# Linear attention and routed experts on one core: the state's sums in 32-row tiles right behind a tile's scores, with the masks, norm tails and opening moved

## The chip, the cores and the metric

The kernel runs on one core of a Trainium2 chip. The metric is the device time of one execution in microseconds; lower is better. The times given are medians of several executions.

## The reference

A block of a transformer on 4 sequences of 2048 rows of 256 numbers, in fp32. Two norms are modulated by vectors worked out from a condition (`mod = silu(c) @ wmod`, six vectors for each sequence). The first half is causal linear attention with 16 heads of 16 numbers, the second a mixture of 8 experts of which each row takes two, with at most 1280 rows for an expert.

```
h = layernorm(x) * (1 + ca) + sa
q, k, v = split(h @ w_qkv.T);  q, k = elu(q) + 1, elu(k) + 1
for each position t:  S += k_t v_t^T;  z += k_t;  o_t = (S^T q_t) / max(z . q_t, 1e-6)
x = x + ga * (o @ w_out.T)
h = layernorm(x) * (1 + cb) + sb
gates = top 2 of softmax(h @ w_router.T), rows past an expert's capacity dropped, weights normalised
x = x + gb * sum_e gate_e * (silu(h @ w_gate.T) @ w_down[e].T)
```

## The kernel before

The rows are cut into 64 tiles of 128 rows, and 4 tiles make a group. The attention part is one loop over slots n (`run_slots`), written out once for each engine: in slot n an engine does its share of tile n, and beside it a quarter of the projections of the next group (stage 1) and of the routing of a group two behind (`routing`: "columns", "first", "second", "place" in the slots 0 to 3 of a group). An order in each engine's `slot_` is written by hand, and semaphores join them. The first 8 slots are negative ones, with an `early` hook for setup work. Behind the attention part comes an expert part of 40 steps, which the change leaves alone.

In a slot TensorE's order is: scores of the tile (`scores`, L1368, 16 calls of 32 rows by 64 columns of weights and 128 moving columns, in the four banks of SCW), transposes of the heads of the tile before and of the keys of the next one (`columns_and_keys`, L1380 and L1386), in slot 0 the transposes of h2 (L1533), a quarter of the projections (L1501 or L1511), the sums from the state (`from_state`, L1398, 8 calls of 64 by 128), the state update (`add_to_state`, L1445, 8 calls of 64 by 64 with 68 moving columns), the sums from the tile (`from_tile`, L1412, 32 calls of 64 by 17), in slot 0 logits (L1552) and stage 1's transposes (L1485), then the output product (L1472), the transposes of the head sums (`head_rows`, L1460) and the other part of the projections. An fp32 product of one call is two records in the trace.

A tile has two halves of 64 rows; the state Sbd is kept for each half. The sums from the state and those from the tile are one accumulation, in OB, which lies in the columns of the same four banks in which the scores stood. So the sums may start only when VectorE has read the scores (`masked_scores`, L994, semaphore sm_done), and the scores of the next tile only when ScalarE has read OB (ot_done). State update: TensorE writes keys times values of both halves to PM, VectorE masks the blocks that belong to one head (L1025, Snew, 272 numbers in a row, semaphore state_read) and adds the halves to the state (L1030, L1036, 136 numbers; sbd_done). PM's banks also hold other results: logits (L1552) and `head_rows` wait for state_read, and in slot 0 the state update waits for ScalarE's two copies of h2's columns (L830, h2t_done).

VectorE's order in a slot is: masks, in slot 0 the row statistics of a group to come (L1059), in slot 2 that norm's tail (`ln_tail`, L1049 to L1052), the state, phi of the projections (L1043), the residual addition (L1159), the normalised heads (`normalise_heads`, L1003 to L1010, An), row statistics (L1163), and in slot 0 the tail of the second norm. The function `between` puts single steps of the routing (`choose`, `place`) among them; place has 9 steps, all in slot 3. GpSimd takes a norm's tail further (L572), modulates the rows (L500, L506), and sends them to their experts (L514); a send waits for a named step of TensorE.

In the opening the modulation vectors come from two products (`modulation`, L1345), the second of them just ahead of slot -1. They are written to the banks of the scores, and VectorE takes them out from slot -1 on (L968 to L979), so that the first scores wait for that; SP sends them to memory and back in all rows (MB), behind the loads of the groups 2 to 7.

## Time and profile before

| | |
|---|---|
| median of 3 executions | 843.34 us (842.8 to 853.23) |
| profiled execution | 848.72 us, its span 847.0 us |
| mean granted TensorE clock | 0.966 |
| TensorE busy | 788.7 us, 93% |
| VectorE / ScalarE / GpSimd busy | 577.3 / 478.8 / 484.0 us |
| first scores of the attention part | 30.12 us into the span |

The profiled execution is one of the longer ones; differences are worked out in its own rows and then set against the median. Busy shares are means over stages, so the rows below are of single stretches and slots.

### The profile page before, as it was taken

What the parts mean: (1) busy time and instruction counts of PE and PEld (TensorE: products, weight loads), DVE (VectorE), ACT (ScalarE), POOL (GpSimd) and SP (SyncE); (2) the same over time, 40 slices, a digit from 0 to 9 for tenths busy, and PEclk for the clock granted to TensorE, in tenths of its full rate; (3) what the DMA queues carried; (4) which work ended last, traced back from release to release, by engine and by line L of the source; (5) the groups of instructions that cost most, each with busy time, mean ns of one, the idle gap of its engine ahead of it and who ended that gap; (6) DMA issues with size and microseconds to landing.
All of it is one profiled execution on the core that took longest, in us unless ns stands there. A gap on an engine that the chain in (4) does not pass through costs nothing.

```text
span 847.0 us, 30958 instructions
## 1 busy us (share of the span) xinstructions
PE 788.7 (93%) x12583; PEld 688.8 (81%) x12583; DVE 577.3 (68%) x1869; ACT 478.8 (57%) x941; POOL 484.0 (57%) x621
## 2 busy tenths in 40 slices
PE   6899899999999999999999998878999997999994
PEld 4687778877877877877877876678999997999993
DVE  4577487878777877877877777522766646767762
ACT  4566467666667667667667664233554553554541
POOL 2203154656666776675766655462765746666764
PEclk9999799999999999999999999759999998999997
DMA  7409823142344132231021121014676655677653
GB/s 282 167 4 337 244 78 115 53 140 77 115 144 136 55 138 90 76 119 68 36 81 54 49 75 39 18 51 150 127 162 147 137 129 112 145 158 158 121 96 38
DMA packets 66844, 95.76 MB, mean 113 GB/s; under 512 B 7682, under 2 KB 48642, under 8 KB 66584
## 3 DMA queue, kind: packets, MB, share of 16 engines
q1 hardware_dynamic: 34136, 50.26, 18.9%
q0 software_dynamic: 21760, 31.66, 16.7%
q10 hardware_dynamic: 10816, 11.96, 4.5%
q8 instruction: 97, 1.59, 0.8%
q14 instruction: 35, 0.29, 0.1%
HBM read 38.97 MB, written 63.36 MB: 121 GB/s over the span
## 4 chain that ended last, share of the span: by engine, by line
PE 77%; DVE 9%; issue 5%; POOL 4%; DMA 3%; ACT 1%; POOLq 0%; SPq 0%; DVEq 0%; ACTq 0%
PE SCW L1727 12%; PE SCW L1398 8%; PE SB L1472 7%; PE SCW L1742 6%; PE SCW L1412 5%; PE PM L1501 5%; PE PJ L1501 3%; PE PM L1445 3%; PE SCW L1368 3%; PE SB L1742 3%; PE PM L1742 3%; PE PJ L1511 3%; PE PM L1460 3%; PE PM L1380 2%; PE PM L1511 2%
## 5 line engine op out<-in xcount | busy, mean ns | idle before, releaser
L514 POOL DMA_INDIRECT slot_rows<-Hrow,sloti x128 | 131.6, 1028 | 102.9 <-PE SCW L1412 60.2
L632 POOL DMA_INDIRECT out<-EX,desti x80 | 125.3, 1566 | 24.2 <-POOL idle L460 11.3
L460 POOL TENSOR_TENSOR idle<-mhalf 128x1 f32<-128x1 f32 x136 | 60.2, 443 | 76.3 <-DVE EX L1298 46.7
L994 DVE TENSOR_TENSOR Sm<-SCW,tri 128x512 f32<-128x512 f32 x128 | 82.1, 682 | 25.7 <-PE SCW L1368 23.9
L851 ACT ACTIVATE OTs<-SCW 128x512 f32<-128x512 f32 x64 | 38.3, 598 | 84.4 <-PE SCW L1412 84.4
L1398 PEld LDWEIGHTS SCW<-QT,Sbd 64*128 64x128 f32 x1024 | 65.3, 192 | 18.7 <-issue 18.0
L564 POOL TENSOR_TENSOR hT<-Sm,hT 128x512 fp32r<-128x512 f32 x30 | 38.3, 1278 | 67.4 <-ACT hT L686 66.6
L1398 PE MATMUL SCW<-QT,Sbd 64*128 64x64 f32 x1024 | 73.8, 284 | 3.0 <-DVE Sm L994 2.8
L701 ACT ACTIVATE N<-X,nb,rs 128x256 f32<-128x256 f32 x128 | 66.3, 592 | 7.5 <-POOL nb L574 4.8
L892 ACT ACTIVATE VA<-SCW 128x512 f32<-128x512 f32 x80 | 47.9, 598 | 38.5 <-PE SCW L1727 35.3
L1742 PE MATMUL SCW<-w_qkv,QS 128*128 128x256 f32 x416 | 62.9, 287 | 4.4 <-DVE QS L1270 4.4
L1025 DVE TENSOR_TENSOR Snew<-PM,headmask 128x272 f32<-128x272 f32 x64 | 28.2, 441 | 52.9 <-PE PM L1445 52.6
L1727 PE MATMUL SCW<-VS,w_g 128*128 128x256 f32 x480 | 61.5, 284 | 0.0
L1727 PE MATMUL SCW<-KS,w_g 128*128 128x256 f32 x480 | 61.4, 283 | 0.0
L1742 PEld LDWEIGHTS SCW<-w_qkv,QS 128*128 128x128 f32 x416 | 57.3, 193 | 4.6 <-issue 4.6
L1727 PEld LDWEIGHTS SCW<-VS,w_g 128*128 128x128 f32 x480 | 58.0, 189 | 0.0
L1727 PEld LDWEIGHTS SCW<-KS,w_g 128*128 128x128 f32 x480 | 57.8, 188 | 0.2 <-DVE KS L1262 0.2
L788 ACT ACTIVATE QM<-QT,parity 128x256 f32<-128x256 f32 x128 | 57.7, 502 | 0.0
L572 POOL TENSOR_TENSOR rs<-vp,mhalf 128x4 f32<-128x4 f32 x31 | 32.5, 1048 | 41.3 <-DVE vp L1052 40.9
L1159 DVE TENSOR_TENSOR X<-X,SB 128x256 f32<-128x256 f32 x64 | 26.7, 418 | 41.2 <-PE SB L1472 40.6
L1412 PE MATMUL SCW<-Sm,VA 64*17 64x64 f32 x4096 | 54.0, 222 | 0.0
L1501 PE MATMUL PJ<-hT,w_qkv 128*128 128x512 f32 x192 | 52.8, 410 | 0.3 <-ACT hT L686 0.3
(253 smaller groups left out, 2025.8 us busy)
## 6 DMA issues: line engine op xcount, KB each, us to landing
Hrow<-slot_rows SPq DMA_DIRECT2D x32, 516.0 KB, 4.4
slot_rows<-erow ACTq DMA_DIRECT2D x1, 10400.0 KB, 41.5
X<-x SPq DMA_DIRECT2D x16, 512.0 KB, 4.8
out<-X SPq DMA_DIRECT2D x16, 512.0 KB, 3.2
QT<-slot_rows SPq DMA_DIRECT2D x8, 516.0 KB, 3.8
Hrow<-MB SPq DMA_DIRECT2D x8, 512.0 KB, 3.5
MB<-mod_rows SPq DMA_DIRECT2D x1, 2048.0 KB
slot_rows<-Hrow,sloti POOLq DMA_INDIRECT x128
```

The source lines that it names most:

```text
L460: pool.tensor_tensor(idle[:, k:k + 1], mhalf[:, 0:1], mhalf[:, 0:1], ALU.add).then_inc(breath, 1)
L514: pool.indirect_dma_start(xe, bass.IndirectOffsetOnAxis(sloti[:, par, k, t:t + 1], 0), Hrow[:, par, t, :], None, bounds_check=last_slot, o ...
L632: pool.indirect_dma_start(out, bass.IndirectOffsetOnAxis(desti[s % 2][:, a:a + 1], 0), Ys[s % 2][:, a, :], None, bounds_check=TOK - 1, oob ...
L701: act.activation(dst, X[:, xt, :], ACT.Identity, scale=rs[:, t:t + 1], bias=nb[:, t:t + 1]).then_inc(s_ready, 1)
L788: act.activation(QM[:, (n + 1) % 2, odd], QT[:, g1 % 2, :, q1 * P:(q1 + 1) * P], ACT.Copy, scale=parity[:, odd:odd + 1]).then_inc(q_masked, 1)
L994: dve.tensor_tensor(Smh(T % 2)[:, 2 * b:2 * b + 2], SCW[:, 2 * b:2 * b + 2, 0:2 * P].rearrange("p r (m i) -> p r m i", i=CH), tri64[:].uns ...
L1398: mm(OB[:, k, b, cc, :], Sbd[part(b), (2 * T + k) % 4, cc, :], QT[part(b), gp, cc, q * P + CH * k:q * P + CH * k + CH], start=(cc == 0), s ...
L1412: last = mm(OB[32 * a:32 * a + SW, k, b, cc, :], VA[part(k), gp, q, head(cc, r, s), :], Smh(T % 2)[part(k), r, 2 * cc + s, :], start=False ...
L1472: last = mm(SB[:, 0:D], ATs[:, cc, :], w_ogs[T // TPB % 2][:, cc, :], start=(cc == 0), stop=(cc == DC - 1))
L1501: last = mm(PJ[m % 2][:], w_qkv[:, wp, cc, (m + 2) % 4 * P:((m + 2) % 4 + 1) * P], hT[:, hp, cc, :], start=(cc + i == 0), stop=(cc == DC - ...
L1727: last = mm(SC[hh][:, (f % 2) * BW:(f % 2 + 1) * BW], w_g[:, wp, cc, f * P:(f + 1) * P], XT[par][:, xp, cc, :], start=(cc + i == 0), stop= ...
L1742: last = mm(((MA, KR), (MD, SB))[par][a][:, 0:D], hid[par][hp][:, f, a * P:(a + 1) * P], WD[k][wp][:, f, :], start=(f + i == 0), stop=(f = ...
```

## The change

The state's sums get columns of their own in the four banks (256 to 383, OB), and are made in tiles of 32 rows and 64 columns with two heads each: 16 calls, right behind the scores of their tile. As two row tiles of the array then write to one bank, the second half of them waits until the scores have run (scores_run). sc_full, for which the masks and some of GpSimd's sends wait, is now given by the last of the sums, and the wait for the masks stands ahead of the sums from the tile. The state has two heads in a block instead of four: Sbd, Snew, headmask and the update's moving operand have half the width, the update has 16 calls of 64 by 32 with 34 moving columns. On VectorE the tail of the second norm goes from the end of slot 0 to behind the masks of slot 1; the last three steps of place go to behind the masks of the next slot 0; and in slot 3 no routing step stands inside `normalise_heads`. In the opening both modulation products run at j = 4, ahead of the first projections, VectorE takes them out there, the masks' setup goes from j = 0 to j = 2, the first statistics wait for a semaphore of one memset instead of all constants, and SP sends MB ahead of the loads of the groups 4 to 7.

```diff
-        OB = SCW[:, :, 0:DC * CH].rearrange("p (k b) (c i) -> p k b c i", k=2, c=DC)
+        OB = SCW[:, :, 2 * P:2 * P + DC * CH].rearrange("p (b k) (c i) -> p k b c i", k=2, c=DC)
...
-            for g in range(2, EARLY):
+            for g in range(2, 4):
                 load_rows_of(g)
...
+            for g in range(4, EARLY):
+                load_rows_of(g)
...
             dve.memset(VA[:], 1.0).then_inc(dve_setup, 1)
+            dve.wait_ge(ones_set, 1)
+
             def early(j):
-                if j == 0:
+                if j == 2:
                     dve.wait_ge(consts, N_CONST)
...
-
-                if j == 7:
 
                     dve.wait_ge(mod_mm, 3)
                     dve.tensor_copy(mod12[:, 0:2, :], OBm).then_inc(gate_fix, 1)
...
-                        if step == "place" and k < 9:
+                        if step == "place" and k < (9 if n >= TILES - 3 else PLACED):
                             place(g, k)
...
                 if tile_ok(n):
                     masked_scores(T)
+                if q == 1 and group_ok(gn - 1):
+                    dve.wait_ge(bn2, 4 * gn)
+                    ln_tail(st2, mv2, vp2, nm2, ag2, vpe2, gn)
+                if step == "columns" and group_ok(g - 1):
+                    for k in range(PLACED, 9):
+                        place(g - 1, k)
...
                 if tile_ok(n):
-                    normalise_heads(T, between, between)
+                    if step == "place":
+                        normalise_heads(T, lambda: None, lambda: None)
+                    else:
+                        normalise_heads(T, between, between)
...
-                if q == 0 and group_ok(gn - 1):
-                    dve.wait_ge(bn2, 4 * gn)
-                    ln_tail(st2, mv2, vp2, nm2, ag2, vpe2, gn)
...
                 if j == 4:
                     modulation(0)
-                if j == 6:
                     modulation(1)
...
-                last.then_inc(sc_full, 1)
+                last.then_inc(scores_run, 1)
...
                 pe.wait_ge(sbd_done, T + 1)
-                for k in range(2):
-                    pe.wait_ge(sm_done, 2 * T + k + 1)
+                for other in range(2):
+                    if other:
+                        pe.wait_ge(scores_run, T + 1)
                     for cc in range(DC):
-                        for b in range(2):
-                            mm(OB[:, k, b, cc, :], Sbd[part(b), (2 * T + k) % 4, cc, :],
-                               QT[part(b), gp, cc, q * P + CH * k:q * P + CH * k + CH], start=(cc == 0), stop=False,
-                               skip_group_check=True)
+                        for r in range(4):
+                            rows, half = slice(32 * r, 32 * r + 32), slice(64 * (r % 2), 64 * (r % 2) + 64)
+                            k = (r + other) % 2
+                            last = mm(OB[half, k, r // 2, cc, :],
+                                      Sbd[rows, (2 * T + k) % 4, cc, :, :].rearrange("p s w -> p (s w)"),
+                                      QT[rows, gp, cc, q * P + CH * k:q * P + CH * k + CH], start=(cc == 0), stop=False,
+                                      skip_group_check=True)
+                last.then_inc(sc_full, 1)
...
+                pe.wait_ge(sm_done, 2 * T + 2)
...
-                        for b in range(2):
-                            h = head(cc, 2 * b, 0)
-                            last = mm(PM[part(b), k, cc * QH * SW:(cc + 1) * QH * SW],
-                                      Kn[part(k), cc * P + CH * b:cc * P + CH * b + CH],
-                                      VA[part(k), gp, q, h:h + QH, :].rearrange("p s w -> p (s w)"),
+                        for r in range(4):
+                            h = head(cc, r, 0)
+                            last = mm(PM[32 * r:32 * r + 32, k, cc * 2 * SW:(cc + 1) * 2 * SW],
+                                      Kn[part(k), cc * P + 32 * r:cc * P + 32 * r + 32],
+                                      VA[part(k), gp, q, h:h + 2, :].rearrange("p s w -> p (s w)"),
                                       start=True, stop=True, skip_group_check=True)
...
-                if tile_ok(n) and n > 0:
-                    scores(n)
+                if tile_ok(n):
+                    if n > 0:
+                        scores(n)
+                    from_state(n)
...
-                if tile_ok(n):
-                    from_state(n)
```

## Rows read from the trace of the kernel before

**Rows 1.** Busy time by stretch: span, PE, PEld, DVE, ACT, POOL, clock, DMA.

```profile
200.00:300.00 100.00, 97.95 (x2036) 80.20 (x2018) 77.78 (x278) 67.31 (x143) 66.36 (x88) 1.00 0.34 117
```

**Rows 2.** The waits from 60 to 450 us: total, times, longest.

```profile
PE PM L1380 <- DVE An L1010: 8.2, 18, 1.2
```

**Rows 3.** Timeline of a slot 3: start, length, engine, line, operation.

```profile
250.57 0.69 PE L1368 MATMUL SCW<-QM,KT 32*64 32x128 f32 x32
...
251.19 0.44 PE L1380 MATMUL PM<-ident,An 128*128 128x128 f32 x2
...
251.37 1.29 DVE L994 TENSOR_TENSOR Sm<-SCW,tri 128x512 f32<-128x512 f32 x2 [0.83 <-PE SCW L1368]
...
253.28 1.11 PE L1398 MATMUL SCW<-QT,Sbd 64*128 64x64 f32 x16
...
254.32 0.47 PE L1445 MATMUL PM<-VA,AK 64*64 64x68 f32 x16
...
254.72 0.83 PE L1412 MATMUL SCW<-Sm,VA 64*17 64x64 f32 x64
```

**Rows 4.** Groups by line from 40 to 450 us: busy us, mean ns, idle before.

```profile
L1398 PE MATMUL SCW<-QT,Sbd 64*128 64x64 f32 x816 | 58.1, 282 | 1.9 <-DVE Sm L994 1.6
...
L1412 PE MATMUL SCW<-Sm,VA 64*17 64x64 f32 x3264 | 42.8, 221 | 0.0
...
L1368 PE MATMUL SCW<-QM,KT 32*64 32x128 f32 x1632 | 35.6, 280 | 2.2 <-issue 2.2
...
L1445 PE MATMUL PM<-VA,AK 64*64 64x68 f32 x816 | 24.1, 234 | 0.0
...
L1030 DVE TENSOR_TENSOR Sbd<-Sbd,Snew 128x136 f32<-128x136 f32 x51 | 19.6, 385 | 0.6
...
L1152 DVE TENSOR_TENSOR Hrow<-gk,esum 128x8 f32<-128x8 f32 x11 | 1.9, 173 | 0.4
```

**Rows 5.** Timeline of the slot 0 behind it.

```profile
258.36 0.69 PE L1368 MATMUL SCW<-QM,KT 32*64 32x128 f32 x32
...
260.69 1.39 DVE L1059 BATCH_NORM_STATS2 st<-X 128x6 f32<-128x256 f32 x4
260.74 0.60 ACT L830 ACTIVATE h2T<-PM 128x512 f32<-128x512 f32 x1
...
261.62 0.47 PE L1445 MATMUL PM<-VA,AK 64*64 64x68 f32 x16
...
262.15 0.44 DVE L1025 TENSOR_TENSOR Snew<-PM,headmask 128x272 f32<-128x272 f32 x1
...
262.77 0.64 PE L1552 MATMUL PM<-h2T,w_r 128*32 128x128 f32 x16
```

**Rows 6.** Timeline of the slot 1 behind it.

```profile
265.69 0.69 PE L1368 MATMUL SCW<-QM,KT 32*64 32x128 f32 x32
...
268.22 1.28 DVE L994 TENSOR_TENSOR Sm<-SCW,tri 128x512 f32<-128x512 f32 x2
...
269.05 1.17 PE L1398 MATMUL SCW<-QT,Sbd 64*128 64x64 f32 x16 [0.16 <-DVE Sm L994]
```

**Rows 7.** Timeline of a slot 0 in which An is late.

```profile
164.21 0.41 PE L1380 MATMUL PM<-ident,An 128*128 128x128 f32 x2 [1.15 <-DVE An L1010]
```

**Rows 8.** Timeline of the opening.

```profile
13.17 3.57 PE L1345 MATMUL SCW<-Sm,cS 128*4 128x512 f32 x4
...
22.77 1.88 PE L1345 MATMUL SCW<-Sm,cS 128*4 128x512 f32 x4
...
28.73 0.67 DVE L968 COPY Hrow<-SCW 4x512 f32<-4x512 f32 x1
...
30.12 0.70 PE L1368 MATMUL SCW<-QM,KT 32*64 32x128 f32 x32 [2.48 <-DVE Hrow L970]
```

**Rows 9.** Timeline of slot 0 of group 2.

```profile
94.82 0.47 PE L1368 MATMUL SCW<-QM,KT 32*64 32x128 f32 x15 [2.20 <-issue]
```

**Rows 10.** Busy time of the stretch around it, columns as in rows 1.

```profile
92.00:107.00 15.00, 12.21 (x181) 9.62 (x179) 4.09 (x11) 6.87 (x14) 1.03 (x1) 0.66 0.63 187
```

More of the change, by code:

```diff
@@ L50 @@
 EARLY = 8
+PLACED = 6
 BIG = 1.0e5
@@ L79, in adaln_block @@
         EX = sb("EX", [P, 2, GW])
-        Snew = sb("Snew", [P, 2, DC * QH, SW])
+        Sbd = sb("Sbd", [P, 4, DC, 2, VW])
+        Snew = sb("Snew", [P, 2, DC * 2, SW])
         OTs = sb("OTs", [P, 2, DC, 2, CH])
@@ L148, in adaln_block @@
             Sm = attention.enter_context(nc.sbuf_tensor("Sm", [P, 2, H, P], F32))
-            Sbd = attention.enter_context(nc.sbuf_tensor("Sbd", [P, 4, DC, QH * VW], F32))
         QS = sb("QS", [P, 2, FC, BW], F32R)
@@ L218, in adaln_block @@
         wipe = sem("wipe")
+        ones_set = sem("ones_set")
         c_silu = sem("c_silu")
@@ L241, in adaln_block @@
         q_masked = sem("q_masked")
+        scores_run = sem("scores_run")
         sc_full = sem("sc_full")
@@ L450, in _ @@
                                base=0, channel_multiplier=-1).then_inc(consts, 1)
[L452 removed]
+            pool.affine_select(out=pairmask[:], in_=pairmask[:], pattern=[[-2 * DH, GT]], compare_op=ALU.is_ge,
                                fill=0.0, base=0, channel_multiplier=1).then_inc(wipe, 1)
             pool.wait_ge(wipe, 1)
[L455 removed]
+            pool.affine_select(out=pairmask[:], in_=pairmask[:], pattern=[[2 * DH, GT]], compare_op=ALU.is_ge,
                                fill=0.0, base=DH - 1, channel_multiplier=-1).then_inc(consts, 1)
@@ L1024, in state @@
                 at_least(dve, sbd_done, t)
-                dve.tensor_tensor(Snew[:], PM[:, :, 0:DC * QH * SW].rearrange("p k (h w) -> p k h w", h=DC * QH),
-                                  headmask[:].unsqueeze(1).to_broadcast([P, 2, DC * QH, SW]), ALU.mult
+                dve.tensor_tensor(Snew[:], PM[:, :, 0:DC * 2 * SW].rearrange("p k (h w) -> p k h w", h=DC * 2),
+                                  headmask[:].unsqueeze(1).to_broadcast([P, 2, DC * 2, SW]), ALU.mult
                                   ).then_inc(state_read, 1)
```

32 lines of the change are left out of this document (13 added, 19 removed).

## Prediction

> **What bounds the kernel now.** I read the windows first. In a steady stretch of the attention part TensorE is busy 97.95 us of 100 at a full clock, VectorE 77.78 [rows 1]. So what counts is how long TensorE's own list of a tile takes, and its few waits. The waits name one of size: the transposes of the normalised heads (L1380) stand 8.2 us in 390 behind VectorE's An, 18 times [rows 2]. The timeline of a slot gives the steps of a tile from start to start [rows 3]: scores 0.62 us (250.57 to 251.19), sums from the state 1.04 (253.28 to 254.32), state update 0.40 (254.32 to 254.72). The groups by line give the mean of one record [rows 4], so the spacing inside a step is (busy - mean) / (count - 1): sums from the state (1.11 - 0.282) / 15 = 0.055 us, state update (0.47 - 0.234) / 15 = 0.016, scores (0.69 - 0.280) / 31 = 0.013, sums from the tile (0.83 - 0.221) / 63 = 0.010. What a step takes beyond count times spacing (1.04 - 16 x 0.055 = 0.16; 0.40 - 16 x 0.016 = 0.15; 0.62 - 32 x 0.013 = 0.20) is the drain where the next step has another tile shape. The sums from the state are dear: 16 records at 0.055, with 64 rows by 128 columns of weights.
>
> **Sums from the state in 32-row tiles.** Calls go from 8 to 16 a tile, records from 16 to 32; each is 32 rows by 64 columns, and four array tiles are in turn. The old state update has the same 64 columns of weights, four array tiles and almost the same moving length (68 for 64): 0.016 us a record. So the step is 32 x 0.016 = 0.50 us. The scores ahead have the same 32*64 shape, so no drain stands between. Scores and sums together: 0.42 + 0.50 + one drain 0.20 = 1.12 us. The new wait on scores_run stands between the two halves. Behind it on TensorE is everything; what it waits for is the end of the last score, at 0.69 us from the slot's start, and the masks now show 0.11 us from such an end to a start on another engine (251.26 to 251.37) [rows 3]: released at 0.80. The first half of the sums covers it until 0.42 + 0.25 = 0.67. Exposed: 0.13 us; bounds 0 (all covered) and 0.3 (the second half starts with an empty array, the first spacing of a step again). I take 0.15, so 1.27 us where 0.62 + 1.04 = 1.66 stood: **0.39 less** a tile.
>
> **State update.** 32 records of 64*32 with 34 moving columns, where 16 of 64*64 with 68 stood. The nearest row is the sums from the tile (same shape, 0.010 a record): 32 x 0.010 = 0.31, and no drain behind it, since that step follows. 0.40 becomes 0.27 to 0.31, and with the initial spacing of the next step saved I take **0.16 less**; bounds 0.1 and 0.2. VectorE's read of it, Snew (0.44 us for 272 elements [rows 5]), has 136, and the two additions half as many: off TensorE's path except in slot 0, below; there I count 0.1.
>
> **The waits that go or come.** L1380 now starts 1.27 us after the scores instead of 0.62, so An has that much longer: the 8.2 us go where An is the last: 0.22 us in each slot 1 (12 times, 2.6), the other 5.6 in the slots 0, 1.15 in the one shown [rows 7]. The masks start when the sums end: 1.27 - 0.20 + 0.28 + 0.11 = 1.4 us into the slot, take 1.29 and end at 2.7. Only the sums from the tile wait for them now, and these come at 3.6 in slots 1 to 3 (1.27, columns 0.4, a projection 1.6, update 0.3). Slack 0.9; no cost. The new early wait of the sums for the state of the tile before (sbd_done) is met: Snew and two additions of 0.385 [rows 4] end 1.8 us behind the update's start (261.62 to 263.4), and the next scores start at 265.69 [rows 5, 6]; 2.3 us of slack, in slot 3, where place steps stand between, some 1.5.
>
> **Slots 2 and 3:** 0.39 + 0.16 = 0.55 less each. **Slot 1** has now the norm tail ahead of the masks: sc_full is there 0.80 us behind the slot's start, at 266.5, the masks start at 268.22 and the sums wait for them (0.16, and the step is 1.17 for 1.11) [rows 6]. The tail behind the masks takes that and the An wait away: 0.16 + 0.06 + 0.22 = 0.45, so 0.55 + 0.45 = 1.0 less. The tail moves from 1.4 to 2.7 us into the slot and ends at 3.5; queued behind it on VectorE are a choose step and Snew, which has until the update at 3.6. GpSimd's power step stands behind a send that waits for sc_full anyway, so it moves by little.
>
> **Slot 0 gives back.** Today the 8 transposes of h2 (1.0 us) and then the sums (1.04) cover ScalarE's two copies of it (the second ends at 261.34), and the update starts at 261.62 [rows 5]. With the sums gone ahead, everything up to the second copy is 0.65 later (end 3.6 us into the slot), TensorE has nothing from 2.8 on, and the update starts at 3.75 instead of 3.26. Then the second thing: logits wait for state_read, that is for VectorE's Snew. VectorE has in line masks (1.4 to 2.7), the three moved tail steps of place (three chained small steps of 173 ns [rows 4] with their waits, 0.6, to 3.3), row statistics 1.39 (to 4.75), Snew 0.33 (to 5.1). Logits start at 5.25 instead of 262.77 - 258.36 = 4.41: **0.85 more**. Against it stands An's wait in the slots 0, 5.6 us / 12 = 0.45 in the mean: normalise_heads no longer has place steps between its own, and L1380 is later. But where An is late, so are the masks and Snew, so I count half: 0.85 - 0.25 = **+0.6**.
>
> **The sum.** A group: -0.55 - 0.55 - 1.0 + 0.6 = -1.5 us. Thirteen groups (3 to 15, the last without projections): -19.5. The first three, without logits in two: -1.8 each, -5.5. The **opening**: the second modulation product (1.88 us) moves ahead of the first projections, where the first product took 3.57 us, so it costs there between 1.88 and 3.57 (I take 2.0, near its price at 22.77, since it is the later part of a longer run of work); it leaves 22.77, and parity and masks leave the path to the first norm (0.7). VectorE's seven steps (from 28.73 on, 3.5 us) go under the projections, and the 2.48 us that the first scores wait for them go [rows 8]. -0.7 + 2.0 - 1.9 - 2.5 = -3, with part of VectorE's phi work then late: bounds -4.5 and -1. SP's rows of groups 4 to 7 now queue behind the modulation rows; they are first read some 30 us later, cover enough. Together -28 us: 848.7 of the profiled execution becomes 820.7. That run lies 5.4 over the median of three, 843.3, so the median becomes **815**.
>
> **Rivals.**
> 1. *The wait moves to VectorE.* If the handshake costs 0.3 and VectorE's line in slot 0 is longer than counted (GpSimd's tensor steps stretch VectorE's additions of 0.30 to 0.7 and more; their mean is 0.385 for it [rows 4]), slot 0 gets +1.4 and each slot 0.15 less: group -0.55 - 0.55 - 1.0 + 1.4 + 0.6 = -0.1. With the opening: about 838. For it: slot 0's times are all on one line. Against: GpSimd sends, and does not compute, in that half of slot 0. Chance 0.16, within 2%.
> 2. *Records have a floor.* If a record with little work costs no less than the 0.025 us that the state update takes now per record (0.40 / 16), sums and update are 0.80 each for 1.04 + 0.40, less 0.2 of drain: nothing gained in slots 2 and 3, 0.45 in slot 1, +1.1 in slot 0: some +10 us less the opening, 850. The 4096 records at a spacing of 0.010 speak against it [rows 4]. Chance 0.03. The Trainium skill (TensorEngine Tiling, Instruction Overhead) says that a matmul with a free dimension of 1 takes as long as one of 60 and that no tiling factor should come from a dimension that is already small; 34 moving columns offend against that.
> 3. *Slower: instruction supply.* In one slot TensorE stood 2.20 us in the middle of a tile's scores with nothing to wait for, and the 15 us around it have a mean granted clock of 0.66 [rows 9, 10]: 2.2 + 15 x 0.34 = 7 us lost. The change adds 16 calls a tile, some 16% more TensorE records in less time. If that starves it, each stop costs 7 us; from four more stops the -28 are gone, at seven it is +21: 865. It happened once in 64 tiles. Chance 0.05. One stop more alone gives 822, one less 808.
> 4. *More than forecast.* If the statistics in slot 0 finish before I count, slot 0 loses only 0.2 and the handshake is free: group -2.4, 800. Chance 0.10.
> 5. *The reordering does nothing*, the 32-row tiles running one after another at 0.055: 32 x 0.055 = 1.76, +0.72 a tile, 860 and more. The scores run 32*64 tiles at 0.013 [rows 4]. Chance 0.02.
>
> **How the numbers follow.** The forecast, 815, has 0.64, with 806 to 826 for its own bounds. The range 802 to 838 leaves out rivals 2, 3, 5 and half of 4. Two per cent is 17 us, about what a measurement of this kernel can tell from no change: faster means under 826.5, which holds the forecast and rival 4, 0.74; within 2% rivals 1, 2 and part of 3, 0.20; slower 0.06.
>
> **What would show it.** Sums from the state: 32 records, the first 0.45 us into the slot. Scores to L1380: 1.27 us. Slots 2 and 3 near 7.15 us, slot 1 near 7.5, slot 0 near 8.2, with L1552 behind Snew and L1445 behind the copies to h2T. L1380 no longer behind An in the waits. First scores near 28 us. I would be wrong if L1412 waits for the masks, if slot 0 grows by over 1.5 us, or if the second half of the sums starts over 0.3 us behind the first.

## The result and the profile after

The changed kernel takes **840.1 us** at the median of 20 runs, the kernel before 845.0 beside it: a ratio of **0.9935**, 95% interval 0.9909 to 0.9962. That is a gain of some 5 us (5.5 by the ratio, 4.9 by the medians): real, but under one per cent. The forecast was 815, 28 us less, with a range of 802 to 838; the result lies outside it. Ratios here and below leave out executions over 1.5% longer than the fastest of their kernel, medians keep them. The profiled execution went from 848.7 to 842.6 us, its span from 847.0 to 840.8.

The page of the changed kernel, its busy line and its chain of work:

```profile
PE 762.5 (91%) x14631; PEld 673.3 (80%) x14631; DVE 551.9 (66%) x1869; ACT 482.2 (57%) x941; POOL 488.2 (58%) x621
...
PE 77%; issue 8%; POOL 5%; DMA 4%; DVE 3%; ACT 2%; POOLq 0%; SPq 0%; ACTq 0%; DVEq 0%
```

TensorE is busy 26 us less (788.7 before), and the time is only 6 us less: 20 us came back as idle time. The chain says where to look: 8% of it is "issue", time in which the engine waited for nothing that the profile shows (5% before). The windows and the waits from 60 to 450 us, as in [rows 1, 2]:

```profile
200.00:300.00 100.00, 95.25 (x2531) 79.00 (x2529) 74.83 (x286) 69.82 (x146) 70.00 (x91) 1.00 0.37 127
```

```profile
PE PM L1457 <- ACT h2T L833: 10.6, 12, 0.9
PE PM L1457 <- issue: 7.4, 12, 0.7
PE SCW L1424 <- issue: 2.9, 2, 2.7
PE PM L1386 <- issue: 2.0, 1, 2.0
PE PM L1497 <- issue: 1.8, 1, 1.8
PE SCW L1374 <- issue: 1.8, 1, 1.8
```

The wait for An, 8.2 us in [rows 2], is gone but for 0.6 us. In its place stand two waits of the state update (L1457), each 12 times, and single stops of 1.8 to 2.7 us. The first wait was forecast (h2T). The second, 0.6 us each, is called "issue", but its length and its count, once in each slot 3, ask for a name. The timeline of slot 3 (scores L1374, sums from the state L1407, An's transposes L1386, projection of V L1523, update L1457, sums from the tile L1424, output L1484) has it, when ScalarE's row is laid beside TensorE's:

```profile
247.97 0.69 PE L1374 MATMUL SCW<-QM,KT 32*64 32x128 f32 x32
248.46 0.79 PE L1407 MATMUL SCW<-QT,Sbd 32*64 32x64 f32 x32
249.19 0.44 PE L1386 MATMUL PM<-ident,An 128*128 128x128 f32 x2
...
251.31 0.60 ACT L807 ACTIVATE VA<-PJ 128x512 f32<-128x512 f32 x1 [0.83 <-PE PJ L1523]
...
252.00 0.36 PE L1457 MATMUL PM<-VA,AK 64*32 64x34 f32 x32 [0.60 <-issue]
252.22 0.87 PE L1424 MATMUL SCW<-Sm,VA 64*17 64x64 f32 x64
253.02 1.13 PE L1484 MATMUL SB<-Sm,AK 128*128 128x256 f32 x4
```

The update starts 0.09 us behind the end of ScalarE's copy of V (251.91), and `add_to_state` waits for that copy when the next tile is the first of a group. So this "issue" is a wait for ScalarE. Slot 0 behind it:

```profile
258.92 0.60 ACT L833 ACTIVATE h2T<-PM 128x512 f32<-128x512 f32 x1
...
259.67 0.36 PE L1457 MATMUL PM<-VA,AK 64*32 64x34 f32 x32 [0.88 <-ACT h2T L833]
259.91 1.35 PE L1424 MATMUL SCW<-Sm,VA 64*17 64x64 f32 x64
...
260.11 1.06 POOL L517 DMA_INDIRECT slot_rows<-Hrow,sloti  x1 [0.51 <-issue]
...
260.42 0.30 DVE L1026 TENSOR_TENSOR Snew<-PM,headmask 128x136 f32<-128x136 f32 x1
...
261.19 0.64 PE L1564 MATMUL PM<-h2T,w_r 128*32 128x128 f32 x16
```

The sums from the tile take 1.28 us here until the next step starts, 0.76 in the kernel before and 0.80 in the slot above. The slot 1 behind it has no wait left:

```profile
264.11 0.69 PE L1374 MATMUL SCW<-QM,KT 32*64 32x128 f32 x32
...
267.42 0.36 PE L1457 MATMUL PM<-VA,AK 64*32 64x34 f32 x32
267.66 0.86 PE L1424 MATMUL SCW<-Sm,VA 64*17 64x64 f32 x64
```

The stops stand each in the middle of a step; of the five of 1.8 us or more, at 34.8, 71.6, 85.4, 101.9 and 356.0 us, three:

```profile
71.63 0.37 PE L1386 MATMUL PM<-ident,An 128*128 128x128 f32 x1 [1.96 <-issue]
...
85.41 0.83 PE L1424 MATMUL SCW<-Sm,VA 64*17 64x64 f32 x38 [2.68 <-issue]
...
101.89 0.92 PE L1374 MATMUL SCW<-QM,KT 32*64 32x128 f32 x23 [1.83 <-issue]
```

A balance of both traces, in us, from the starts of the scores of tiles 0, 4, 12, 60 and 63 (slots in the middle: mean from one start of scores to the next, over the 12 slots of a kind among n = 12 to 59):

| | before | after | difference | forecast |
|---|---|---|---|---|
| first scores at | 30.12 | 27.77 | -2.3 | -3 |
| n0 to n3 | 31.9 | 33.8 | +1.9 | -1.8 |
| n4 to n11 | 69.0 | 71.7 | +2.7 | -3.6 |
| n12 to n59 | 380.5 | 370.1 | -10.4 | -18 |
| of it a slot 0 | 7.76 | 8.27 | +0.51 | +0.6 |
| a slot 1 | 8.47 | 7.34 | -1.13 | -1.0 |
| a slot 2 | 7.69 | 7.27 | -0.42 | -0.55 |
| a slot 3 | 7.79 | 7.96 | **+0.17** | **-0.55** |
| n60 to n62 | 26.0 | 24.6 | -1.4 | -1.5 |
| behind them | 309.4 | 312.9 | +3.4 | 0 |

Some 22 us are missing: 9 of them in the slots 3 from n12 on, 10 in the first 12 slots, 3 at the end. The experiments go after each. All ratios below are to the kernel before. Slot means ("in the mean") are over the 12 slots of a kind among n = 12 to 59; single slots are named.

### The profile page after: what moved, and what is told of

Same layout as the page of the kernel before. It is cut to its first block, busy times and chain, and to the rows that moved or that the text cites. A ratio compares the mean times of both kernels' runs of the same rounds, so it can differ in the third digit from the quotient of the medians.

```text
span 840.8 us, 35024 instructions
## 1 busy us (share of the span) xinstructions
PE 762.5 (91%) x14631; PEld 673.3 (80%) x14631; DVE 551.9 (66%) x1869; ACT 482.2 (57%) x941; POOL 488.2 (58%) x621
## 4 chain that ended last, share of the span: by engine, by line
PE 77%; issue 8%; POOL 5%; DMA 4%; DVE 3%; ACT 2%; POOLq 0%; SPq 0%; ACTq 0%; DVEq 0%
PE SCW L1739 11%; PE SB L1484 7%; PE SCW L1424 6%; PE SCW L1754 6%; PE PJ L1513 5%; PE PM L1513 5%; PE SCW L1374 5%; PE SCW L1407 4%; PE PM L1472 3%; PE PJ L1523 3%; PE PM L1754 3%; PE SB L1754 3%; PE PM L1457 2%; PE PM L1386 2%; PE PM L1523 2%
## 5 line engine op out<-in xcount | busy, mean ns | idle before, releaser
L517 POOL DMA_INDIRECT slot_rows<-Hrow,sloti x128 | 135.5, 1058 | 60.4 <-issue 28.4
L1424 PE MATMUL SCW<-Sm,VA 64*17 64x64 f32 x4096 | 64.2, 223 | 6.6 <-issue 5.4
L1739 PE MATMUL SCW<-KS,w_g 128*128 128x256 f32 x480 | 63.1, 289 | 0.0
L1424 PEld LDWEIGHTS SCW<-Sm,VA 64*17 64x17 f32 x4096 | 51.8, 93 | 12.0 <-issue 9.0
L800 ACT ACTIVATE AK<-PM 128x512 f32<-128x512 f32 (+1 forms) x66 | 38.7, 586 | 39.3 <-PE PM L1392 38.4
L1513 PE MATMUL PM<-hT,w_qkv 128*128 128x512 f32 x192 | 53.9, 417 | 0.0
```

Of the source, the lines that this page charges most:

```text
L517: pool.indirect_dma_start(xe, bass.IndirectOffsetOnAxis(sloti[:, par, k, t:t + 1], 0), Hrow[:, par, t, :], None, bounds_check=last_slot, o ...
L1424: last = mm(OB[32 * a:32 * a + SW, k, b, cc, :], VA[part(k), gp, q, head(cc, r, s), :], Smh(T % 2)[part(k), r, 2 * cc + s, :], start=False ...
L1513: last = mm(PJ[m % 2][:], w_qkv[:, wp, cc, (m + 2) % 4 * P:((m + 2) % 4 + 1) * P], hT[:, hp, cc, :], start=(cc + i == 0), stop=(cc == DC - ...
L1739: last = mm(SC[hh][:, (f % 2) * BW:(f % 2 + 1) * BW], w_g[:, wp, cc, f * P:(f + 1) * P], XT[par][:, xp, cc, :], start=(cc + i == 0), stop= ...
```

## The experiments

**Slot 3.** The sums from the tile need only the masks, and these end at 2.7 us; so they can cover the copy of V.

```diff
+                if q == 3 and tile_ok(n):
+                    from_tile(n)
                 if n >= -1 and tile_ok(n + 1):
                     add_to_state(n, g, routed, step)
-                if tile_ok(n):
+                if q != 3 and tile_ok(n):
                     from_tile(n)
```

> Changed kernel with one step moved: in slot 3 alone the sums from the tile run ahead of the state update, so that their 0.8 us cover ScalarE's copy of the V projection. Theory A (the cover that the sums from the state gave to that copy is what slot 3 lost): slot 3 goes from 7.95 us to 7.25, 15 slots, 10 us less than the changed kernel, about 0.982 of the kernel before. Rival B (the gain is lost to stops in TensorE's instruction supply and a fuller VectorE, not to this wait): the next waits take it over, slot 3 stays over 7.7, under 3 us less, about 0.990. Rival C: the masks end too late for the earlier place (they end 2.7 us into the slot, the sums from the tile would start at 3.3), so it costs nothing.

Measured: 830.9 us, **0.9834** (0.9789 to 0.988). Slot 3 has a mean of 7.29 us. Its rows:

```profile
247.62 0.60 ACT L807 ACTIVATE VA<-PJ 128x512 f32<-128x512 f32 x1 [0.83 <-PE PJ L1523]
...
247.65 0.83 PE L1424 MATMUL SCW<-Sm,VA 64*17 64x64 f32 x64
248.33 0.41 PE L1457 MATMUL PM<-VA,AK 64*32 64x34 f32 x32
248.67 1.13 PE L1484 MATMUL SB<-Sm,AK 128*128 128x256 f32 x4
```

The copy runs from 247.62 to 248.22 beside the sums, and the update does not wait. Theory A has it: exchanging two calls gives more than the whole change gave.

**The sums from the state back at the old place in slots 0 and 3** (`LATE` true for q = 0 and 3). Here VectorE's masks wait for `scores_run`, and the sums for the masks, since both use the same banks.

```diff
                     if n > 0:
                         scores(n)
-                    from_state(n)
+                    if not LATE(q):
+                        from_state(n)
...
+                if LATE(q) and tile_ok(n):
+                    pe.wait_ge(sm_done, 2 * n + 2)
+                    from_state(n)
                 if n >= -1 and tile_ok(n + 1):
```

> Changed kernel with the sums from the state (still in 32-row tiles) back at their old place in slots 0 and 3, behind the masks and ahead of the state update; slots 1 and 2 as changed. Theory A (the placement loses in slots 0 and 3 what the small tiles gain, since ScalarE's copies of h2 and of V lose their cover): slot 3 goes from 7.95 to 7.25 and slot 0 from 8.06 to 7.4, 15 x 0.7 + 13 x 0.65 = 19 us less than the changed kernel, about 0.971 of the kernel before. Rival B (slot 0 is set by VectorE's row statistics and Snew, whatever TensorE does): slot 0 stays at 8.0, 10 us less, about 0.982. Rival C (stops in the instruction supply grow with any faster stretch): under 5 us less.

Measured: 831.9 us, 0.9833 (0.9797 to 0.9868), less than half of what theory A gives. Slot 3 came down to 7.47. Slot 0 is 7.50 at its best (n12, n32), but 8.29 in the mean: the waits from 120 to 500 us hold L1391 behind An again, 6.1 us in 7 waits, up to 1.3 each. So the early sums hide a late An; putting them back uncovers it.

**The old place in all slots** (`LATE` true for every q).

> Changed kernel with the sums from the state, in 32-row tiles, at the old place in all slots; only the tile form, the norm tail, the place steps and the opening are changed then. If the placement gives nothing by itself, slots 1 and 2 stay at 7.25 to 7.4 (the handshake of 0.15 goes, one more drain of 0.15 to 0.2 comes) and the time is that of the version with two slots moved back, 0.97 to 0.975 of the kernel before. If the placement is what gains in slot 1 and 2 (no wait for An), these are 0.2 to 0.4 longer each, 30 slots, 6 to 12 us more than that version.

Measured: 855.2 us, **1.0124** (1.0087 to 1.0162), outside all that was expected: slots 1 and 2 are 8.41 and 7.73 us. In the rows of a slot 1 (n33) the 32 sums from the state take 0.63 us, as they should, but the sums from the tile 1.23, beside a send of GpSimd's:

```profile
307.09 1.30 PE L1429 MATMUL SCW<-Sm,VA 64*17 64x64 f32 x64
...
307.23 0.99 POOL L522 DMA_INDIRECT slot_rows<-Hrow,sloti  x1 [1.63 <-PE SCW L1412]
...
308.32 1.13 PE L1489 MATMUL SB<-w_og,AK 128*128 128x256 f32 x4
```

GpSimd's sends wait for `sc_full`, which the change moved from the end of the scores to the end of the sums; with the sums late, a send is released right ahead of the small records. In slot n10 of the same run, where no group is sent yet, the same step takes 0.78. That asks for the send to be moved alone. The changed kernel shows the same by degrees: a slot 2 has 0.64 us of a send beside its sums from the tile, and they take 0.93 us in nearly all of them, a slot 3 has none and takes 0.80. The send is moved first in slot 0 of the changed kernel:

```diff
                 if paced and q == 0:
+                    pool.wait_ge(state_read, T + 2)
                     send_row(0, 0)
```

> Changed kernel with GpSimd's first send of a slot 0 held until VectorE has read the state (Snew). Theory (the send, which the moved place steps have pushed from the slot's first 2 us onto the state update and the sums from the tile, slows TensorE's small records there: 64 of them take 1.22 us from groups 3 on, 0.79 without a send): the logits come 4.7 instead of 5.14 us into slot 0, 12 slots, 5 us less, 0.987. Rival (the 64 records are slow because they follow a wait and 32 others, whatever GpSimd does): logits at 5.14, 0.9935.

Measured: 829.9 us, **0.9817** (0.9762 to 0.9872). The logits come at 4.68 us in place of 5.14 (4.7 was expected) and a slot 0 without a late An or a stop is 7.60 long instead of 8.06. Twelve of these are 5.5 us; the means of slot 0, 7.95 for 8.27, give 3.8, with a stop of 1.8 us in n20 of this trace. By the medians it is 10 us, more than the trace explains. The rows of n32:

```profile
289.45 0.82 PE L1425 MATMUL SCW<-Sm,VA 64*17 64x64 f32 x64
290.24 0.65 PE L1565 MATMUL PM<-h2T,w_r 128*32 128x128 f32 x16
...
290.48 1.07 POOL L517 DMA_INDIRECT slot_rows<-Hrow,sloti  x1 [1.37 <-DVE Snew L1027]
```

Then in the version with the sums late everywhere, with the sends of slots 1 and 2 back where the kernel before had them:

```diff
-                    pool.wait_ge(sc_full, T + 1)
+                    pool.wait_ge(scores_run, T + 1)
                     send_row(1, 0)
```

(and the same ahead of `send_row(2, 1)`)

> The version with the sums from the state in 32-row tiles at their old place in every slot, and GpSimd's sends of slots 1 and 2 released by the end of the scores, as in the kernel before, where they were released by the end of the sums, 0.2 us ahead of the state update. Theory (a send that runs beside the 32 and 64 small records of the update and the sums from the tile slows them by 0.43 us): the sums from the tile take 0.79 us again in slots 1 and 2, which go from 8.41 and 7.73 us to 8.0 and 7.3, 24 slots, 10 us less: 1.000 of the kernel before instead of 1.012. Rival (the 64 records are slow because 64 small ones stand right ahead of them): no change, 1.012.

Measured: 840.7 us, **0.9943** (0.9909 to 0.9977). That is better than the 1.000 expected: one semaphore's name is worth 1.8% of that version. Slots 1 and 2 go from 8.41 and 7.73 to 8.14 and 7.24 in the mean; the mean of slot 1 holds a stop in n29 (11.71); n13, n33 and n37 are 7.68.

```profile
306.31 0.99 POOL L522 DMA_INDIRECT slot_rows<-Hrow,sloti  x1
...
307.64 0.85 PE L1429 MATMUL SCW<-Sm,VA 64*17 64x64 f32 x64
308.42 1.13 PE L1489 MATMUL SB<-w_og,AK 128*128 128x256 f32 x4
```

0.78 us with the send over ahead of it, 1.23 beside it. The rival, that 64 small records behind 64 others are slow, falls: they stand in the same row here. The two traces also tell the send's row on GpSimd from its transfer. The packets of the sends (the profile's queue "software_dynamic") run beside the 0.78 us here, 22 of them between 307.64 and 308.42, and none runs beside the 1.23 us of the run before, from 307.09 to 308.32. So the stretching goes with the send's row, and not with the data on its way. Other work of GpSimd's does not do it either: a TENSOR_TENSOR of 1.06 us, from 307.32, stands beside the 0.78 us here.

The two runs also price the early place itself. A slot 2 has 7.16 us with the sums late and no send beside the small records, 7.12 with them early (n10) and 7.27 with them early and a send: nothing to gain. A slot 1 has 7.68 for 7.25, 0.43, which is mostly its wait for An.

**Slot 0's other waits.** Sums from the tile ahead of the update in slot 0 too:

> Changed kernel with the sums from the tile ahead of the state update in slots 0 and 3 (the run before had it in slot 3 alone). If slot 0 is set by the logits' wait for VectorE's Snew, which stands behind 1.4 us of row statistics, filling TensorE's wait for the copies of h2 gives nothing: the update still starts near 3.7 us into the slot, the logits near 5.15, slot 0 stays at 8.05. If instead TensorE's wait for the copies (0.88 us) is what slot 0 lost, slot 0 goes to 7.3.

Measured, one execution: 823.2 us. Neither of the two came: slot 0 is 7.67 without a late An (8.18 in the mean), the logits start at 4.75. Then VectorE's statistics behind Snew as well:

```diff
-                if q == 0 and group_ok(gn + 2) and gn >= 1:
-                    ln1_stats(G, gp)
...
                     state(n, between, lambda: None)
+                if q == 0 and group_ok(gn + 2) and gn >= 1:
+                    ln1_stats(G, gp)
```

> As the run before, and VectorE's row statistics of slot 0 (1.4 us) moved behind Snew and its two additions. Theory (slot 0 is two waits, one behind the other: the update for ScalarE's copies, the logits for Snew behind the statistics): the logits start near 4.45 us into the slot instead of 5.15, slot 0 goes from 8.05 to 7.35, 13 x 0.7 = 9 us less than with slot 3 alone put right: about 822 us, 0.972 of the kernel before. Rival: the later statistics make VectorE late in slot 1 or the next An late, and half of it comes back: 0.977.

Measured: 823.8 us, 0.9709 (0.9607 to 0.9811), but not for the reason given: Snew starts 4.40 us into n32, 4.41 in the run ahead.

```profile
280.75 0.30 DVE L1026 TENSOR_TENSOR Snew<-PM,headmask 128x136 f32<-128x136 f32 x1 [1.20 <-PE PM L1457]
...
281.10 0.64 PE L1564 MATMUL PM<-h2T,w_r 128*32 128x128 f32 x16 [0.74 <-DVE Snew L1026]
```

VectorE is idle for 1.20 us ahead of Snew, waiting for the update, which by its row began at 280.00. In the run ahead the statistics ended just when the update was done; moving them gave nothing. My theory for this edit fell. With the send held as well (and the fill in pieces, last experiment) Snew comes at 4.15 to 4.18 and the logits at 4.50 in the slots without a late An: 0.52 us behind the update's start where it was 0.75 with the send beside it, so the send seems to stretch the update too.

**The stops.** What a stop waits for stands among the DMA transfers, in the queue that the profile calls "instruction": 97 transfers of 16 KB in the kernel before, 113 in the changed one. The stop that ends at 85.41 has one in it, from 83.03 to 84.08. The view of the DMA queues from 82.73 to 85.41 has:

```profile
q8 instruction: 1, 0.02, 2.4%
```

It ends 1.33 us ahead of the stop's end; for the stops at 34.8, 71.6, 101.9 and 356.0 it is 1.46, 1.48, 1.52 and 1.63. In the traces of all runs there are 75 stops of over 1.0 us named "issue" between 30 and 515 us, and 73 of them end 1.2 to 1.7 us behind the end of such a transfer (the other two, 2.0 and 2.5, stand in the narrow fill below). So in the stops TensorE waits for instructions. In the five of the changed kernel the transfer itself takes 0.9 to 1.1 us, no longer than elsewhere: it comes late and not slowly, and what made it late the traces don't show.

A stop can cost more than its length. Right behind the stop of 2.68 us, in which TensorE was idle, the granted clock is 0.50, the lower of the two levels (1.2 GHz); so it is behind those at 34.8, 71.6 and 101.9, and not behind the one at 356.0:

```profile
85.00:91.50 6.50, 6.09 (x52) 4.48 (x51) 1.61 (x5) 1.39 (x3) 5.26 (x10) 0.50 1.09 333
```

The stops between 58 and 104 us lie in the 10.65 MB fill of the expert rows, one transfer. It was cut into ten, one in each of the slots 1 to 10, in both kernels.

```diff
+                if 1 <= n <= 10:
...
+                    act.dma_start(fill[:, 8 * n - 8:8 * n, :], erow[:].to_broadcast([P, 8, D + 4])).then_inc(init_out, 16)
```

> Changed kernel with the 10.5 MB fill of the expert rows sent in ten pieces, one in each of the slots n = 1 to 10, where one transfer stood at n = 3. Theory A (TensorE's instructions are fetched late while the fill takes all queues, and that makes the stops of 2 to 2.7 us between 69 and 102 us): the stops of over 1.5 us there go, slots n5, n6 and n8 come from 10.64, 12.81 and 11.23 to 8 or less, 8 to 11 us less: 0.982 to 0.985 of the kernel before. Rival B (the stops come from the instructions themselves, wherever they are fetched): the same number of stops, same time. Rival C: the pieces spread the stops over ten slots, no gain.

> Kernel before with the same ten pieces. Theory A: it had two stops in that stretch and slot n8 of 14.88 us; with the pieces n8 comes to about 8, 6 to 7 us less: 0.992. If the changed kernel gains 3 us or more on top of that by the same edit, the change pays more for the fill than the kernel before did. Rival: equal gains in both, so the fill is no part of what the change missed.

Measured: the changed kernel 834.7 us, 0.987 (0.9807 to 0.9933); the kernel before 839.9, 0.9919 (0.9881 to 0.9957). So some 5.5 and 7 us: equal within the intervals, so that by the times alone the rival of the second text stands. The traces say why. In the kernel before no stop is left, n4 to n11 take 61.8 us instead of 69.0. In the changed one they take 66.8 instead of 71.7, and three stops remain, 1.68 us in n6 (at 75.7) and these two, in n6 and n10:

```profile
81.76 0.61 PE L1424 MATMUL SCW<-Sm,VA 64*17 64x64 f32 x38 [2.15 <-issue]
...
113.55 0.77 PE L1424 MATMUL SCW<-Sm,VA 64*17 64x64 f32 x57 [1.78 <-issue]
```

Next the fill as one transfer, but of the last four columns of each row alone: as many pieces, 0.16 MB.

```diff
-                    act.dma_start(xe[:, 0:D + 4].rearrange("(p n) r -> p n r", p=P),
-                                  erow[:].to_broadcast([P, SLOTS // P, D + 4])).then_inc(init_out, 16)
+                    act.dma_start(xe[:, D:D + 4].rearrange("(p n) r -> p n r", p=P),
+                                  erow[:, :, D:D + 4].to_broadcast([P, SLOTS // P, 4])).then_inc(init_out, 16)
```

> Changed kernel with a fill that writes only the last four columns of each expert row (weights, index, mark) instead of all 260: 0.16 MB for 10.65, as one transfer at the same place; the rest of a row that nobody sends is never stored. Theory A (the stops between 58 and 102 us are instruction fetches that wait behind the fill's bytes): no stop of over 1.5 us between 60 and 130 us, the slots n4 to n11 take 61 us together instead of 71.7, 9 us less in all: 0.983 of the kernel before. Rival B (the stops belong to the instructions and come at other places too): n4 to n11 over 66 us, stops near n6 and n10 as with the ten pieces, 0.988.

> Kernel before with the same narrow fill. Theory A: n4 to n11 take 61.8 us as with the ten pieces (69.0 with the whole fill), no stops: 0.991. The difference between the two kernels in these eight slots is then what the change gains there when nothing disturbs it, and the difference with the whole fill what the fill took of it; if the changed kernel gains 2 us or more beyond what this one gains, part of the missed gain is the fill's.

Measured: the changed kernel 836.2 us, 0.988 (0.9832 to 0.9928), the kernel before 848.0, 1.0016 (0.998 to 1.0052). The bytes are gone and the stop is not. It is one now, in n5 of both, and longer in the changed kernel (first fence) than in the one before (second):

```profile
75.90 0.37 PE L1386 MATMUL PM<-ident,An 128*128 128x128 f32 x1 [5.89 <-issue]
```

```profile
76.74 0.62 PE L1412 MATMUL SCW<-Sm,VA 64*17 64x64 f32 x28 [3.10 <-issue]
```

The length is not the changed kernel's own, for in the best version below, with the same fill, the one stop there is 2.5 us. So the fill does not need its bytes to hold TensorE; many small pieces do it too, and theory A, as written, was wrong. That it is the number of pieces in one transfer fits the ten parts, but no run varied that number alone. The other seven slots of the changed kernel are undisturbed in that run (67.2 - 15.4 = 51.8 us); with n5 at the 7.12 that it takes with the ten pieces, n4 to n11 would be 58.9. Against 61.8 in the kernel before that is 2.9 less, near the forecast's 3.6. The whole fill thus took 71.7 - 58.9 = 12.8 us of the changed kernel and 69.0 - 61.8 = 7.2 of the kernel before in the two profiled executions, and the difference, 5.6, is most of the miss of 6.3 in these slots. The two prices come out of the rows: three stops are 6.5 us, and a mean granted clock of 0.87 over the 46 us from 58 to 104 costs some 46 x 0.13 = 6.0 us (my estimate, as if all of it went by the clock), 12.5 in all; in the kernel before 2.2 us of a stop and 46 x 0.09 = 4.1. The same windows of the changed kernel, the kernel before, and the kernel before with ten pieces; the clock is the third number from the end:

```profile
58.00:104.00 46.00, 37.46 (x893) 30.64 (x885) 21.63 (x69) 23.67 (x46) 11.22 (x19) 0.87 0.88 269
```

```profile
58.00:104.00 46.00, 42.23 (x878) 34.58 (x877) 28.30 (x77) 26.78 (x52) 12.06 (x19) 0.91 0.88 268
```

```profile
58.00:104.00 46.00, 44.62 (x948) 36.73 (x949) 32.73 (x95) 31.27 (x62) 15.86 (x23) 1.00 0.58 187
```

More records in the kernel before, to see whether these alone bring stops (a half of the scores made twice, 16 records a tile. The text on record says "as many as the change adds"; the change adds 16 calls, which are 32 records, so this is half as many):

> Kernel before with the first half of each tile's scores made twice (16 records more a tile, as many as the change adds; same operands, same result). Theory A (TensorE's instructions come late more often when there are more of them to a microsecond): the 16 records cost their 16 x 0.013 = 0.21 us a tile, 13 us, and stops of over 1 us with nothing to wait for come more often, five or more between 30 and 520 us where the kernel before has one and the version with the fill in pieces none: 20 us or more in all, 1.024 or higher. Rival B (the stops of the changed kernel come from its placement or its opening): 13 us, 1.016, one or two stops.

Measured: 854.8 us, 1.0101 (1.0041 to 1.0162): less than both, though rival B's 1.016 is just inside the interval. In slots 0 and 1 the records hide in the wait for An (7.57 and 8.49 in the mean), in slots 2 and 3 they cost 0.28 and 0.31. The rest of the loss is in the first 12 slots: n0 to n3 take 34.0 us, 2.1 more, and n4 to n11 73.8, 4.8 more; the stretch of the fill has three stops of over a microsecond for one, and from n12 to n59 there is none. So in this trace 16 records more a tile bring no stops where nothing else loads. That they bring more of them in the fill is not shown: the kernel before with the new opening alone (next experiment) has two there, 1.96 and 2.90 us, without a record more.

**The opening**, alone in the kernel before, and taken out of the changed kernel:

> Kernel before with the reordered opening alone. Theory A (the first scores come 2.3 us earlier and nothing else changes): 0.997 of the kernel before, with the lead of 2.3 us kept through the first group. Rival B (the reordering puts the work of the first tile into the loads of the second modulation rows, where TensorE's instructions come late): a stop of about 2 us in the first slot, the lead gone by the second tile, ratio 1.000.

> Changed kernel with the opening in the old order. Theory A (the new opening lets the first tile run into the loads of the modulation rows, where its many instructions come late: slot n0 is 10.8 us there, 7.6 before): first scores at 30 us, n0 to n3 in 30 us instead of 33.8, so the opening gives nothing: the same time as the changed kernel, 0.9935 within 0.002. Rival B (the opening gives its 2 to 3 us all the same): 2 to 3 us slower, 0.997. Rival C (the opening costs): 0.991.

Measured: alone 844.2 us, 0.9995 (0.9966 to 1.0024); the changed kernel with the old one 844.2, 0.9985 (0.9947 to 1.0024), where with the new one it has 0.9935. With the new opening alone the lead of 1.9 us at the first scores shrinks to 0.7 by n1 and is 1.6 at tile 63. With the old opening the changed kernel has a stop too, 2.58 us in n1, and n0 to n3 take 34.4 us: the new opening is not the cause of the loss there. It is worth between 0 and 4 us. The first scores vary by as much as the gain: over the traces of all runs they come at 28.7 to 30.1 us with the old opening and at 26.7 to 28.9 with the new one.

**The norm tail of slot 1**, alone in the kernel before:

> Kernel before with the norm tail of h2 behind the masks of slot 1, and nothing else. By the prediction's terms slot 1 loses the wait for the masks (0.16 and 0.06) and the wait for An (0.22) and goes from 8.50 to 8.05, the other slots stay: 12 x 0.45 = 5 us. If the whole 1.25 us that slot 1 lost in the changed kernel is the tail's, it goes to 7.8 or below; if the tail only moves the wait to Snew, it stays at 8.50.

Measured, one execution: 837.0 us. A slot 1 is 8.21 instead of the 8.50 of most slots 1 before, 0.29 less (0.26 by the means) where 0.45 was expected. The waits:

```profile
264.42 0.41 PE L1380 MATMUL PM<-ident,An 128*128 128x128 f32 x2 [0.22 <-DVE An L1010]
...
266.37 1.11 PE L1398 MATMUL SCW<-QT,Sbd 64*128 64x64 f32 x16
```

The wait for the masks of [rows 6] is gone, the wait for An stays; that one needs the sums ahead of it.

**All together**: exchange in slots 0 and 3, statistics, send held, ten pieces; and the same with the narrow fill.

> Sums from the tile ahead of the update in slots 0 and 3, row statistics behind Snew, the send held, the fill in ten pieces, together. Slot 0 at 7.3 to 7.4 us where no An is late, slots 1 to 3 at 7.25 to 7.3, the fill's stops gone: 813 to 818 us, 0.965 of the kernel before. Rival: the held send makes GpSimd and with it VectorE late in slot 1 and 2, or the stops come elsewhere: 0.972, no better than without the last two edits.

> The best version so far (sums from the tile ahead of the update in slots 0 and 3, statistics behind Snew, the send held) with the narrow fill in place of the ten pieces. Theory A: n4 to n11 in 58 us, no stops there, 808 to 813 us, 0.96 of the kernel before. Rival B: stops as with the pieces, 817, 0.966.

Measured: 817.2 us, 0.9657 (0.959 to 0.9723), and 820.4 us, 0.9591 (0.951 to 0.9672), with six executions from 808.6 to 828.4 us. Both beat both kernels, and are not told apart from each other. Four slots in the middle take 29.8 us for 31.7 before and 30.8 in the change as made.

## Why the prediction was wrong, point by point

- **The step that failed** is in the sum: "Slots 2 and 3: 0.39 + 0.16 = 0.55 less each". In slot 0 I asked what the moved sums had covered, in slot 3 not. There they stood between the first half of V's projection and the update, 1.04 us over a copy of 0.60. Without them the update waits 0.60 by its row, and slot 3 gave +0.17 for -0.55: 9 us over n12 to n59, 11 in 15 slots. Shown, by exchanging the two calls (slot 3 at 7.29). The one term was charged in slots 2 and 3 alike, and in slot 3 it was wrong in its sign.
- **The tile form was right.** Scores to An's transposes: 1.27 forecast, 1.22 measured; the first sum 0.49 us into the slot, forecast 0.45. Update to sums from the tile: 0.40 became 0.22 to 0.24, 0.16 to 0.18 less. Against rival 2 stand 32 records of 34 columns in 0.24 us, 0.0075 each. Rivals 2 and 5 fall. The Trainium skill (TensorEngine Tiling (Array Packing), Instruction Overhead) says that a matmul with a free dimension of 1 takes as long as one of 60. The trace does not bear out a price for each record in a row of them: twice the records with 34 columns instead of 68 took 0.24 us for 0.40.
- **The waits.** An's transposes wait 0.6 us in all for 8.2, as forecast; the masks have their slack; slot 1 has -1.13 for -1.0. Its An term was mis-sized: I took the 0.22 of the wait's row, but from the scores to the transposes a slot 1 with An late has 1.18 us (264.42 - 263.24 with the tail alone) where slot 3 has 0.62 [rows 3]. Of the 0.56 between, 0.17 are a transpose of the logits that only slot 1 has (1.38 for 1.21 in the changed kernel), so the wait was worth 0.39. The tail's own part was 0.29 for 0.22, and form and place 0.57 for 0.55 (7.69 to 7.12 in n10). Together 1.25, which is what a slot 1 without another delay shows: 8.50 to 7.25.
- **Slot 0** gave +0.51 for +0.6, by another way than I wrote. The wait for h2's copies came as forecast (update at 3.73 in the slot shown, 3.62 in most, 3.75 forecast). Behind it I had Snew at 4.75 and the logits behind Snew; it came at 4.4 to 4.5, and the logits waited for the sums from the tile, which a send of GpSimd's stretched by 0.45 to 0.5. The prediction said "GpSimd sends, and does not compute, in that half of slot 0" as a point *against* a loss. That was the wrong way round: the moved place steps hold the send back until it falls on the update and the sums. A right total from two errors of opposite sign.
- **Slot 2** gave -0.42 for -0.55. In n10, where no send is, it is 7.12 as forecast; from n14 on 7.27, with 0.64 us of a send beside the sums from the tile, which take 0.93 us for 0.79.
- **Rival 3, instruction supply**, had 0.05 and was the second part of the miss. Against the forecast n0 to n3 lost 3.7 us and n4 to n11 6.3, of which three slots 3 are 2.2 and the rest, some 8, stops in the first loads and in the fill, with the lower clock behind them. That TensorE lacks instructions in them is shown by the instruction transfers that end ahead of each. The rival's price, 7 us for each stop, was too high here: three took 12.8, 4.3 each. That a fill of 0.16 MB in as many pieces brings a stop too, I had not considered. Why the changed kernel has more of them stays open: it has more TensorE instructions (14631 matmul records for 12583, 113 instruction transfers for 97), but half as many added to the kernel before brought none outside the fill.
- **The opening** gave 2.3 us at the first scores for 3, and in the time between 0 and 4; not settled.
- **Behind tile 63** the changed kernel took 3.4 us more, in code that the change leaves alone. Over all profiled executions the last 40 steps took between 259.5 and 270.5 us from their start: 260.8 to 267.5 in the six traces made from the kernel before, 259.5 to 270.5 in the thirteen made from the changed one. One trace of each can't say whose it is; it stays open.

The sum, by the rows of the table: 0.7 for the opening, 3.7 and 6.3 for the first 12 slots, 7.6 for the next 48 (8.6 in slot 3, 1.6 in slot 2, less 2.7 in slots 0 and 1), 0.1 and 3.4 behind them: 21.8 of the 28 - 6 = 22 that were missing.

## What to carry to other kernels

Before work is moved off its place, list every wait that stood behind it, in every variant of the loop body, not only in the one where the loss is plain; each needs a new cover, and one may lie ready in the next call. A wait that the profile calls "issue" and that comes back at the same place in every round has a cause in the program: look for what ended on another engine a tenth of a microsecond ahead of it. One that stands in the middle of a step is another matter; look at the instruction transfers. A semaphore whose increment moves with the work carries the engines that only used it as a clock: look up all its waiters. And where an engine works at hundredths of a microsecond a record, look at what GpSimd and the DMA queues do in the same tenths.

## What the runs showed of the hardware

- A GpSimd send (DMA_INDIRECT, 0.97 to 1.07 us) that runs beside 64 TensorE records of 64 by 17 stretches these from 0.78 to 1.23 us, in three kernels, with no semaphore that would make them wait; with 0.64 us of it beside them they take 0.93. The logits' larger matmuls show no such thing (0.57 to 0.58 us from their start to the next step, with or without it). The stretching goes with the send's row and not with its transfer (slots n33 of the two versions with the sums late). The Trainium skill (Perfetto Trace Analysis, DMA Instruction — SWDGE (GPSIMD)) says that the end of such a row is the end of descriptor generation, not of the transfer. The profile agrees: the page of the changed kernel has 3.0 us from issue to landing for rows of 1.06. By what way the row touches TensorE no run here shows.
- In a fill of 10240 pieces of 16 bytes TensorE stops once, for 3.1 us (kernel before) or 5.9 (changed kernel), in the middle of a step (2.5 in the best version); with pieces of 1040 bytes once for 2.2 us (kernel before) or three times for 1.8 to 2.7 (changed kernel). In ten parts of 1024 pieces the kernel before had no stop, the changed one three of 1.7 to 2.2 us.
- Such stops end 1.2 to 1.7 us behind a 16 KB transfer of the queue "instruction" in 73 of 75 cases, and the granted clock behind some of them is the lower level (0.50 from 85.0 to 91.5 us of the changed kernel, behind a stop of 2.68 us).
- TensorE's small records go down to 0.0075 us from one to the next when the calls go to several tiles of the array in turn.
